# A mixture-of-experts layer staged over three batches, with one ring of four PSUM banks

## The chip, the cores and the metric

The kernel runs on one core of one Trainium2 chip. The metric is the device time of one launch in microseconds (us), the median of several runs. Every number below is of that core: TensorE (PE; PEld is its weight load, which overlaps it), VectorE (DVE), ScalarE (ACT), GpSimd (POOL) and the DMA queue that SyncE (SP) feeds.

## What is computed

Four transformer layers in a row over 16 batches of 256 tokens of width 128, with a context of 1601 rows per batch. The first layer, the third and the fourth are attention layers; they run in two programs with the name prefixes `pa_` and `pb_`, and nothing of them is touched. The case is about the second layer, whose buffers begin with `moe_`. Cut to what matters:

```python
nx = _layer_norm(x, ln_gamma, ln_beta)
q = nx @ Wq ; k = prototype_bank @ Wk ; v = prototype_bank @ Wv      # bank: 1601 rows
weights = softmax(einsum('bth,bph->btp', q, k) * H ** (-0.5))
evidence = einsum('btp,bph->bth', weights, v)
combined = concatenate([nx, evidence, anchor], axis=-1)
router_probs = softmax(combined @ router_W + router_b)
h = silu(einsum('btc,ecr->bter', combined, e_w1) + e_b1)              # 3 experts, 256 hidden
expert_out = einsum('bter,erh->bteh', h, e_w2) + e_b2
routed = sum(expert_out * router_probs[..., None], axis=-2)
g = sigmoid(silu(combined @ gate_w1 + gate_b1) @ gate_w2 + gate_b2)
return x + g * (routed @ out_w + out_b)
```

## The kernel before

`expert_layer` works on one batch at a time in units; each unit is a few matmuls of PE into one PSUM bank and the move of that bank to SBUF by ACT or DVE. Tokens come as two tiles (QT = 2) of 128, the context as 13 tiles of 128 rows (the last has 65), in four groups of at most four tiles.

The front of a batch is: `ln` (layer norm statistics on DVE, with the inverse root by 15 small operations, L155 to L168, and `xn`, L1319), `xt` (two transposes, L1536), `q` (L1539) and `qk` (times Wk transposed, L1542), `c0` to `c3` (transposes of the context, L1548), `s0` and `s1` (scores of token tile 0 and 1 in four banks of 400 columns, L1528; row maxima on DVE, L1333; exponentials on ACT, L1456; then sum, reciprocal and a diagonal matrix of the reciprocals, L1339 to L1345), `p00` to `p13` (probabilities transposed and divided at once by a matmul with that diagonal, L1564, moved by L1421 on ACT and L1255 on DVE), `pc` (context times probabilities, 13 accumulating matmuls, L1554) and `ev` (times Wv, L1557).

The back is: `r` (router logits, L1575, softmax on DVE and ACT, L1359 to L1372), `h0` to `h2` (an expert's hidden layer, L1580; ACT reads the bank as `hz`, L1480, takes the tanh, L1483, and DVE multiplies, L1382), `g1` (L1583), `e0` and `e1` (the experts' second matmuls for one token tile, L1589, each expert with a bias matmul of one row, L1590; DVE weights and adds, L1399 and L1401), `g2` (L1594, bias L1595; tanh L1487, then L1407 on DVE), `rt` (two transposes, L1600), `o` (L1604, bias L1605; DVE multiplies by the gate, L1412; POOL adds x, L1506; SP stores, L1285).

The front uses two banks in turn, the back two others. Every engine walks one list in program order: `walk` puts the front of batch b+1 between the units of the back of batch b, so two batches are in flight. The exponentials of a token tile stand right behind its scores on ACT, and its maxima, sum and diagonal in one piece on DVE. x has three buffers, the context one (`cin`), the probabilities before the transpose one per token tile.

A wait names a unit's count on a semaphore: `f_full` and `b_full` count what PE has filled, `f_free` and `b_free` what has been moved out.

## Time and profile before

| | us |
|---|---|
| median of 3 runs | 5992.55 |
| lowest and highest | 5966.28, 6003.84 |
| the profiled execution | 5973.85 |
| its span on the core | 5972.1 |

The span has three parts: the program `pa_` up to about 1978 us, the expert layer from there to 2834 us, and the program `pb_`. Over the whole span PE is busy for 84%, DVE for 68%, ACT for 62% and POOL for 27%. Only the middle part is changed. A busy PE is not PE at its peak, since the ends of matmuls are modelled and a weight load or a drain can stand between two of them: the difference between two starts is the better price. A float32 matmul shows as two instructions, a transpose as one.

### The profile page before, as it was taken

The numbers are of one execution on the slowest core, as the hardware profiler recorded it, in microseconds if no ns is written. First come the engines' busy times: TensorE is split into PE (matmuls) and PEld (weight loads), VectorE is DVE, ScalarE is ACT, GpSimd is POOL, SyncE is SP. The second block draws the span as 40 slices with busy tenths as digits, with TensorE's granted clock in tenths as the row PEclk, the third lists the DMA queues.
The fourth block names the chain that finished last, engine by engine and source line by source line (L and its number), as shares of the span: only waits on it lengthen the run. The fifth ranks groups of instructions, "written<-read, shape, count | busy, mean of one in ns | idle before, by whom it ended". The sixth has DMA issues, their size and how long they took to land.

```text
span 5972.1 us, 124563 instructions
## 1 busy us (share of the span) xinstructions
PE 5013.7 (84%) x48593; PEld 2443.0 (41%) x48593; DVE 4034.0 (68%) x8799; ACT 3691.2 (62%) x5043; POOL 1624.9 (27%) x2594
## 2 busy tenths in 40 slices
PE   3688888888888688888598888888888898888887
PEld 1233333333433466666233333333334343333333
DVE  3487877777776233332588878787877777777774
ACT  1376767667767233332277777777777777777775
POOL 2434343343321000000423232323222322322321
PEclk8699999999999788888699999999999999999998
DMA  1221111211110100000211212121212111111110
GB/s 42 60 61 46 51 53 50 59 43 47 51 34 24 34 16 22 23 23 17 68 43 58 60 50 61 50 61 50 61 50 62 48 51 44 52 49 42 53 42 7
DMA packets 362968, 271.18 MB, mean 45 GB/s; under 512 B 47905, under 2 KB 324990, under 8 KB 362384
## 3 DMA queue, kind: packets, MB, share of 16 engines
q1 hardware_dynamic: 362384, 263.23, 15.5%
q8 instruction: 387, 6.34, 0.4%
q14 instruction: 197, 1.61, 0.1%
HBM read 86.96 MB, written 12.78 MB: 17 GB/s over the span
## 4 chain that ended last, share of the span: by engine, by line
PE 31%; DVE 8%; ACT 6%; POOL 4%; issue 4%; SPq 0%; DMA 0%; ACTq 0%; POOLq 0%
PE pb_obank L914 11%; PE pb_dbank L927 7%; DVE pb_c_maxs L599 6%; ACT pb_probs L668 4%; PE pb_aunit L890 4%; PE pb_aunit L961 2%; PE pb_aunit L968 2%; POOL pb_c_cin L789 1%; PE pb_aunit L1001 1%; PE pb_dbank L975 1%; DVE pb_z_maxs L599 1%; POOL pb_c_hg L852 1%; PE pb_aunit L995 1%; POOL pb_c_cs_y L785 0%; ACT pb_c_ksp L712 0%
## 5 line engine op out<-in xcount | busy, mean ns | idle before, releaser
L599 DVE TENSOR_REDUCE pb_c_maxs<-pb_dbank 128x1 f32<-128x512 f32 (+1 forms) x3584 | 2050.6, 627 | 633.3 <-PE pb_dbank L927 621.2
L668 ACT ACTIVATE pb_probs<-pb_aunit 128x1024 f32<-128x1024 f32 (+1 forms) x1792 | 1756.0, 1025 | 460.7 <-PE pb_aunit L890 364.6
L599 DVE TENSOR_REDUCE pa_c_maxs<-pa_dbank 128x1 f32<-128x512 f32 (+1 forms) x1792 | 1028.6, 627 | 395.6 <-PE pa_dbank L927 390.4
L668 ACT ACTIVATE pa_probs<-pa_aunit 128x1024 f32<-128x1024 f32 (+1 forms) x960 | 943.0, 1025 | 263.6 <-PE pa_aunit L890 190.8
L927 PE MATMUL pb_dbank<-pb_c_kst,pb_c_qst 62*128 62x512 bf16 (+1 forms) x4096 | 880.1, 343 | 141.5 <-DVE pb_c_maxs L599 77.0
L914 PE MATMUL pb_obank<-pb_probs,pb_c_vaug 128*9 128x256 f32 x13312 | 890.2, 382 | 6.6 <-ACT pb_probs L668 6.5
L890 PE MATMUL pb_aunit<-pb_c_qst,pb_c_kst 64*128 64x256 bf16 x6144 | 595.8, 273 | 53.3 <-ACT pb_probs L668 21.9
L927 PEld LDWEIGHTS pb_dbank<-pb_c_kst,pb_c_qst 62*128 62x128 bf16 x4096 | 248.6, 93 | 778.4 <-DVE pb_c_maxs L599 563.7
L927 PE MATMUL pa_dbank<-pa_c_kst,pa_c_qst 62*128 62x512 bf16 (+1 forms) x2048 | 449.0, 354 | 61.5 <-DVE pa_c_maxs L599 24.2
L914 PE MATMUL pa_obank<-pa_probs,pa_c_vaug 128*9 128x256 f32 x6656 | 461.2, 393 | 0.8 <-ACT pa_probs L668 0.7
L914 PEld LDWEIGHTS pb_obank<-pb_probs,pb_c_vaug 128*9 128x9 f32 x13312 | 276.1, 90 | 371.9 <-issue 177.3
L890 PEld LDWEIGHTS pb_aunit<-pb_c_qst,pb_c_kst 64*128 64x128 bf16 x6144 | 258.6, 95 | 242.0 <-ACT pb_probs L668 84.4
L890 PE MATMUL pa_aunit<-pa_c_qst,pa_c_kst 64*128 64x256 bf16 x3072 | 300.9, 278 | 25.7 <-ACT pa_probs L668 16.7
L927 PEld LDWEIGHTS pa_dbank<-pa_c_kst,pa_c_qst 62*128 62x128 bf16 x2048 | 123.3, 95 | 390.0 <-DVE pa_c_maxs L599 257.1
L599 DVE TENSOR_REDUCE pa_z_maxs<-pa_dbank 128x2 f32<-128x512 f32 x256 | 164.1, 686 | 115.3 <-PE pa_dbank L927 113.9
L1506 POOL TENSOR_TENSOR moe_xo<-moe_y,moe_xin 128x256 f32<-128x256 f32 x16 | 11.6, 723 | 844.2 <-DVE moe_y L1412 844.2
L914 PEld LDWEIGHTS pa_obank<-pa_probs,pa_c_vaug 128*9 128x9 f32 x6656 | 140.2, 91 | 195.7 <-issue 101.7
L803 POOL TENSOR_TENSOR pb_c_kf<-pb_c_kf,pb_c_ksp 128x1024 f32<-128x1024 f32 x64 | 114.3, 1787 | 311.1 <-ACT pb_c_ksp L712 311.1
L890 PEld LDWEIGHTS pa_aunit<-pa_c_qst,pa_c_kst 64*128 64x128 bf16 x3072 | 129.1, 96 | 117.3 <-ACT pa_probs L668 44.2
L599 DVE TENSOR_REDUCE pb_z_maxs<-pb_dbank 128x2 f32<-128x512 f32 x256 | 164.6, 685 | 10.5 <-PE pb_dbank L927 8.7
L1564 PE MATMUL moe_bank_f<-moe_diag,moe_pr 128*128 128x128 f32 (+1 forms) x832 | 136.9, 320 | 35.5 <-DVE moe_pt L1255 28.5
L1456 ACT ACTIVATE moe_pr<-moe_bank_s,moe_nm 128x400 f32<-128x400 f32 (+1 forms) x128 | 74.3, 594 | 132.5 <-DVE moe_nm L1337 132.5
(460 smaller groups left out, 6864.7 us busy)
## 6 DMA issues: line engine op xcount, KB each, us to landing
pb_c_kst<-pb_c_ksp SPq DMA_DIRECT2D x384, 200.1 KB
pa_c_kst<-pa_c_ksp SPq DMA_DIRECT2D x192, 200.1 KB
pb_c_cin<-in_ctx SPq DMA_DIRECT2D x32, 768.0 KB
pa_c_cin<-in_ctx SPq DMA_DIRECT2D x16, 768.0 KB
moe_cin<-in_ctx SPq DMA_DIRECT2D x16, 768.0 KB
pb_c_qst<-pb_c_qsp SPq DMA_DIRECT2D x384, 32.0 KB
...
```

Of the source, the lines that this page charges most:

```text
L599: dve.tensor_reduce(dst, dbank[N % RING_D][:, 0:cnt * width].rearrange("p (s c) -> p s c", s=cnt), AX.X, ALU.max).then_inc(d_free, 1)
L668: act.activation(probs[u % RING_P][0:rows].rearrange("p a i q -> p (a i q)"), src[0:rows, :], ACT.Exp, scale=HD ** -0.5).then_inc(a_free, 1)
L789: pool.tensor_scalar(s.cin[0:rows, t, :], s.cin[0:rows, t, :], s.cs_m[0:rows, t:t + 1], s.cs_y[0:rows, t:t + 1], ALU.add, ALU.mult).then_i ...
L803: pool.tensor_tensor(s.kf[:, part], s.kf[:, part], s.ksp[:, 0, part], ALU.subtract).then_inc(s.k_r, 1)
L852: pool.tensor_tensor(s.hg[:], s.hg[:], s.z[:], ALU.mult).then_inc(s.g_p, 1)
L890: ins = pe.matmul(dst[:, par * 512 + h * NQ:par * 512 + (h + 1) * NQ], s.kst[b2][lo:lo + ROWS, pair, t * P:(t + 1) * P], s.qst[b2][lo:lo + ...
L914: ins = pe.matmul(obank[32 * h4:32 * h4 + HD + 1, half * NQ:(half + 1) * NQ], s.vaug[i % 2][:, t, 4 * q + h4, :], src, start=(t == 0), sto ...
L927: ins = pe.matmul(dbank[nd[tok, s.key, i, par] % RING_D][:, col:col + width], s.qst[b2][lo:lo + MAX_ROW, p, qt * P:(qt + 1) * P], s.kst[b2 ...
L961: ins = pe.matmul(dst[:, at - t0 * P:at - t0 * P + width], w.wkp[:], src[:, at:at + width], start=True, stop=True)
L968: ins = pe.matmul(dst[0:rows, (t - t0) * P:(t - t0 + 1) * P], (s.srct if s.has_ctx else s.xmt)[:, t * P:t * P + rows], w.wv[:], start=True ...
L1456: act.activation(pr[qt][:, at:at + width], sbank[c][:, 0:width], ACT.Exp, bias=nm[:, qt:qt + 1], scale=D ** -0.5, accum_out=sums[:, qt, c: ...
L1564: ins = pe.matmul(dst[0:rows, (t - t0) * P:(t - t0 + 1) * P], pr[qt][:, t * P:t * P + rows], diag[qt][:], start=True, stop=True)
```

## The change

The expert layer has a new list of stages, `expert_stages`, which all engines walk. In the body numbered b, a token (name, offset) works on batch b + offset: `xt`, `qk`, `c`, the scores `s` and the exponentials of token tile 0 (`x`, 0) on batch b+2; the exponentials of token tile 1 (`x`, 1), `p`, `dn`, `rb`, `pc` and `ev` on b+1; the back on b; `ln` on b+3. There are 19 bodies, the first and the last only partly filled.

- All units use one ring of four banks in turn, 27 uses for each batch; a unit waits until the use four before it has been moved. Each score bank is still apart.
- `q` is gone: Wq times Wk transposed is made once, and `qk` is one matmul from `nxt`.
- `p` is a plain transpose of unscaled probabilities. `dn` makes sum, reciprocal and diagonal for both token tiles at once; `rb` is two matmuls of a matrix of ones with the diagonals, which spreads the reciprocals over all rows (`recb`); the product `pc` is multiplied by it as DVE moves it.
- The biases of `e`, `g2` and `o` are split once, by `bias_parts` on DVE, in three bf16 parts in rows 0, 32 and 64 of `brows`. One bf16 matmul over 384 or 256 columns opens each bank in place of the six or two matmuls of one row.
- The inverse root is one power on POOL, which also makes `xn` and the affine step of `g2`.
- x has five buffers, the context three, the probabilities two, `nxt` three. The loads of the context are issued before the second part of the constants, and from then on after the product of three batches earlier.
- The softmax of the router is split: the exponential stands ahead of `hz` of expert 1 on ACT, the rest ahead of DVE's part of it.

```diff
+def expert_stages(nb, groups):
+
+    plan = [("xt", 2), ("p", 1, 0, 0), ("h", 0, 0), ("qk", 2), ("x", 1, 1), ("p", 1, 0, 1), ("dn", 1), ("r", 0), ("h", 0, 1),
+            ("c", 2, 0), ("p", 1, 0, 2), ("p", 1, 0, 3), ("rb", 1), ("h", 0, 2), ("c", 2, 1), ("p", 1, 1, 0), ("c", 2, 2),
+            ("g1", 0), ("p", 1, 1, 1), ("c", 2, 3), ("s", 2, 0), ("p", 1, 1, 2), ("p", 1, 1, 3), ("e", 0, 0), ("e", 0, 1), ("g2", 0),
+            ("x", 2, 0), ("ln", 3), ("pc", 1), ("s", 2, 1), ("rt", 0), ("ev", 1), ("o", 0)]
+    out = []
+    for b in range(-3, nb):
+        for tok in plan:
+            n = b + tok[1]
+            if 0 <= n < nb:
+                out.append((tok[0], tok[2:], n))
+    return out
...
-    FRONT = ["xt", "q", "qk", "c0", "c1", "c2", "c3"] + [f"p{qt}{g}" for qt in range(QT) for g in range(len(TG))] + ["pc", "ev"]
-    BACK = ["r", "h0", "h1", "h2", "g1", "e0", "e1", "g2", "rt", "o"]
...
+    RING = ("xt", "qk", "c", "p", "rb", "pc", "ev", "r", "h", "g1", "e", "g2", "rt", "o")
+    nu = {}
+    for k, arg, n in PROG:
+        if k in RING:
+            nu[k, arg, n] = len(nu)
...
-        wq, wk, wkt, wv = (sb(n, [P, D]) for n in ("wq", "wk", "wkt", "wv"))
+        wq, wk, wqt, wkt, wqk, wv = (sb(n, [P, D]) for n in ("wq", "wk", "wqt", "wkt", "wqk", "wv"))
...
+        xin = [sb(f"xin{i}", [P, QT, D]) for i in range(5)]
+        cin = [sb(f"cin{i}", [P, KT, D]) for i in range(3)]
...
-        pr = [sb(f"pr{i}", [P, KEYS]) for i in range(QT)]
-        sums, tot, rec = sb("sums", [P, QT, NCH]), sb("tot", [P, QT]), sb("rec", [P, QT])
+        pr = [[sb(f"pr{j}{i}", [P, KEYS]) for i in range(QT)] for j in range(2)]
...
+        recb = sb("recb", [P, NQ])
...
+        def filled(k, arg, n):
+
+            return u_full, nu[k, arg, n] + 1
+
+        def moved(k, arg, n):
+
+            N = nu[k, arg, n]
+            return u_free[N % RING_U], N // RING_U + 1
...
+            for dst, src, slow in consts_list[0:6]:
+                sp.dma_start(dst, src, allow_slow_non_contiguous=slow).then_inc(consts, 16)
             load_c(0)
+            for dst, src, slow in consts_list[6:]:
+                sp.dma_start(dst, src, allow_slow_non_contiguous=slow).then_inc(consts, 16)
             load_x(1)
+            load_c(1)
+            for part in range(3):
+                row = 32 * part
+                sp.dma_start(braw[row:row + 1, 0:EXPERTS, :], w["e_b2"].rearrange("(o e) n -> o e n", o=1)).then_inc(b_in, 16)
+                sp.dma_start(braw[row:row + 1, EXPERTS, :], w["gate_b2"].rearrange("(o n) -> o n", o=1)).then_inc(b_in, 16)
+                sp.dma_start(braw[row:row + 1, EXPERTS + 1, :], w["out_b"].rearrange("(o n) -> o n", o=1)).then_inc(b_in, 16)
...
+                load_c(n + 3)
                 store(n)
+                load_x(n + 4)
+                load_cols(n + 2)
...
+            def bias_parts():
+                dve.wait_ge(b_in, 9 * 16)
+                dve.wait_ge(b_zero, 1)
+                link = Chain(dve, b_step, 0)
+                for part in range(3):
+                    row = slice(32 * part, 32 * part + 1)
+                    src = braw
+                    for _ in range(part):
+                        link(dve.tensor_copy(bpart[row], src[row]))
+                        link.join()
+                        link(dve.tensor_tensor(brest[row], src[row], bpart[row], ALU.subtract))
+                        link.join()
+                        src = brest
+                    dve.tensor_copy(brows[row, 0:EXPERTS + 1, :], src[row, 0:EXPERTS + 1, :]).then_inc(b_set, 1)
+                    dve.tensor_copy(brows[row, EXPERTS + 1, :], src[row, EXPERTS, :]).then_inc(b_set, 1)
+                    for t in range(QT):
+                        dve.tensor_copy(brows[row, EXPERTS + 2 + t, :], src[row, EXPERTS + 1, :]).then_inc(b_set, 1)
...
+                    if n == 0:
+                        bias_parts()
...
+                elif k == "dn":
+                    dve.wait_ge(s_exp, (n + 1) * QT * NCH)
+                    if n:
+                        dve.wait_ge(*filled("rb", (), n - 1))
+                    dve.tensor_reduce(tot[:], sums[n % 2][:], AX.X, ALU.add).then_inc(s_sum, 1)
+                    dve.wait_ge(s_sum, n + 1)
+                    dve.reciprocal(rec[:], tot[:]).then_inc(s_rec, 1)
+                    dve.wait_ge(s_rec, n + 1)
+                    for qt in range(QT):
+                        dve.tensor_scalar(diag[qt][:], ident[:], rec[:, qt:qt + 1], None, ALU.mult).then_inc(s_diag, 1)
...
+                elif k == "pc":
+                    dve.wait_ge(*filled(k, arg, n))
+                    dve.wait_ge(*moved("rb", (), n))
+                    if n:
+                        dve.wait_ge(*filled("ev", (), n - 1))
+                    dve.tensor_tensor(pct[:], src[:, 0:NQ], recb[:], ALU.mult).then_inc(free, 1)
...
+                elif k in ("h", "g1"):
+                    j = arg[0] if k == "h" else EXPERTS
+                    if j == 1:
+                        link = Chain(dve, r_dve, n * R_PER)
+                        link.n = 2
+                        dve.wait_ge(r_exp, n + 1)
+                        link(dve.reduce_sum(ls[:], le[:], AX.X))
+                        link.join()
+                        link(dve.reciprocal(ls[:], ls[:]))
+                        link.join()
+                        link(dve.tensor_tensor(rp[:], le[:], ls[:].unsqueeze(2).to_broadcast([P, QT, EXPERTS]), ALU.mult))
+                        link.join()
+                    dve.wait_ge(h_tanh, HIDDEN * n + j + 1)
...
+                elif k == "x":
+                    qt = arg[0]
+                    act.wait_ge(s_neg, n * QT + qt + 1)
+                    if n >= 2:
+                        act.wait_ge(*filled("p", (qt, len(TG) - 1), n - 2))
+                        act.wait_ge(s_sum, n - 1)
+                    for c, (at, width) in enumerate(CH):
+                        act.activation(pr[n % 2][qt][:, at:at + width], sbank[c][:, 0:width], ACT.Exp, bias=nm[:, qt:qt + 1], scale=SCALE,
+                                       accum_out=sums[n % 2][:, qt, c:c + 1]).then_inc(s_exp, 1)
...
+                elif k in ("h", "g1"):
+                    j = arg[0] if k == "h" else EXPERTS
+                    if j == 1:
+                        act.wait_ge(r_dve, n * R_PER + 2)
+                        wait(act, r_dve, n * R_PER)
+                        act.activation(le[:], lx[:], ACT.Exp).then_inc(r_exp, 1)
+                    if j == 0:
+                        act.wait_ge(cols_in[n % 2], (n // 2 + 1) * COL_LOADS)
+                    act.wait_ge(*filled(k, arg, n))
+                    wait(act, h_out, HIDDEN * n + j)
...
+                if k == "ln":
+                    pool.wait_ge(ln_st, 2 * QT * (n + 1))
+                    pool.tensor_scalar(rs_v[:], ag[:, :, 1], EPS, None, ALU.add).then_inc(ln_p, 1)
+                    pool.tensor_scalar(rs_m[:], ag[:, :, 0], -1.0, None, ALU.mult).then_inc(ln_p, 1)
+                    pool.wait_ge(ln_p, 3 * n + 2)
+                    pool.tensor_tensor(rs_y[:], rs_v[:], mhalf[:], ALU.pow).then_inc(ln_p, 1)
+                    pool.wait_ge(ln_p, 3 * n + 3)
+                    if n:
+                        pool.wait_ge(*filled("xt", (), n - 1))
+                    for t in range(QT):
+                        pool.tensor_scalar(xn[:, t, :], xin[n % 5][:, t, :], rs_m[:, t:t + 1], rs_y[:, t:t + 1], ALU.add, ALU.mult).then_inc(x_ln, 1)
...
+            for k, arg, n in PROG:
+                if k in RING:
+                    N = nu[k, arg, n]
+                    dst = ubank[N % RING_U]
+                    wait(pe, u_free[N % RING_U], N // RING_U)
...
+                    pe.wait_ge(*moved("xt", (), n))
+                    ins = pe.matmul(dst[:, 0:NQ], wqk[:], nxt[n % 3][:], start=True, stop=True)
...
+                elif k == "p":
+                    qt, g = arg
+                    t0, cnt = TG[g]
+                    pe.wait_ge(s_exp, (n * QT + qt + 1) * NCH)
+                    for t in range(t0, t0 + cnt):
+                        rows = LAST if t == KT - 1 else P
+                        ins = pe.transpose(dst[0:rows, (t - t0) * P:(t - t0 + 1) * P], pr[n % 2][qt][:, t * P:t * P + rows], ident[:])
+                elif k == "rb":
+                    pe.wait_ge(s_diag, (n + 1) * QT)
+                    for qt in range(QT):
+                        ins = pe.matmul(dst[:, qt * P:(qt + 1) * P], ones[:], diag[qt][:], start=True, stop=True)
...
-                    wait(pe, s_norm, after(n, QT, qt))
-                    for t in range(t0, t0 + cnt):
-                        rows = LAST if t == KT - 1 else P
-                        ins = pe.matmul(dst[0:rows, (t - t0) * P:(t - t0 + 1) * P], pr[qt][:, t * P:t * P + rows], diag[qt][:], start=True, stop=True)
...
+                elif k == "e":
+                    qt = arg[0]
+                    pe.wait_ge(b_set, 12)
+                    pe.wait_ge(h_out, HIDDEN * n + EXPERTS)
+                    pe.matmul(dst[:, 0:EXPERTS * D], ones_b[:], brows[:, 0:EXPERTS, :].rearrange("p e d -> p (e d)"), start=True, stop=False)
                     for e in range(EXPERTS):
                         for r in range(2):
-                            pe.matmul(dst[:, e * D:(e + 1) * D], hh[:, e, r, qt * P:(qt + 1) * P], ew2[:, e, r, :], start=(r == 0), stop=False)
-                        ins = pe.matmul(dst[:, e * D:(e + 1) * D], ones[:], eb2[0:1, e, :], start=False, stop=True)
+                            ins = pe.matmul(dst[:, e * D:(e + 1) * D], hh[:, e, r, qt * P:(qt + 1) * P], ew2[:, e, r, :], start=False, stop=(e == EXPERTS - 1 and r == 1))
```

## Rows read from the trace of the kernel before

**Rows 1.** Fifteen periods in one window: us, busy times and instructions, granted clock, DMA share, GB/s
```profile
2080.00:2830.00 750.00, 634.59 (x2962) 491.63 (x2962) 260.52 (x879) 230.91 (x589) 10.85 (x15) 0.87 0.08 21
```
**Rows 2.** The tile moe_y: durations of 16 instructions in ns, first and last start
```profile
L1412 DVE TENSOR_TENSOR moe_y<-moe_bank_g,moe_g x16: 424/425/426, 2080.0 to 2830.0; 128x256 f32<-128x256 f32 x16
```
**Rows 3.** PE's longest wait of one period: us, times, longest
```profile
PE moe_bank_s L1528 <- DVE moe_ct L1326: 2.1, 1, 2.1
```
**Rows 4.** Windows of one period, columns as in rows 1
```profile
2290.00:2297.00 7.00, 6.01 (x19) 4.89 (x20) 0.98 (x6) 1.04 (x3) 0.09 (x1) 0.53 0.61 156
2297.00:2324.00 27.00, 21.77 (x113) 16.19 (x111) 14.15 (x49) 12.34 (x32) 0.00 (x0) 1.00 0.00 1
```
**Rows 5.** Timeline, PE in one period: start us, us, engine, line, operation, instructions
```profile
2281.51 5.85 PE L1554 MATMUL moe_bank_f<-moe_pt,moe_cin 128*128 128x256 f32 x26 [0.47 <-DVE moe_pt L1257]
...
2299.92 1.04 PE L1548 MATMUL moe_bank_f<-moe_ident,moe_cin 128*128 128x128 f32 x8
...
2300.79 0.60 PE L1580 MATMUL moe_bank_g<-moe_nxt,moe_ew 128*128 128x256 f32 x2
...
2305.39 2.93 PE L1528 MATMUL moe_bank_s<-moe_ct,moe_qk 128*128 128x401 f32 x8 [2.06 <-DVE moe_ct L1326]
...
2313.83 0.61 PE L1589 MATMUL moe_bank_g<-moe_ew,moe_hh 128*128 128x128 f32 x4
...
2314.37 0.48 PE L1590 MATMUL moe_bank_g<-moe_eb,moe_ones 1*128 1x128 f32 x2
...
2314.79 0.71 PE L1589 MATMUL moe_bank_g<-moe_ew,moe_hh 128*128 128x128 f32 x4
...
2328.79 2.05 PE L1564 MATMUL moe_bank_f<-moe_diag,moe_pr 128*128 128x128 f32 x16
...
2330.68 0.38 PE L1600 MATMUL moe_bank_g<-moe_ident,moe_rt 128*128 128x128 f32 x2
```
**Rows 6.** Timeline, ACT and DVE around scores and a hidden layer, same columns
```profile
2297.57 0.84 ACT L1480 ACTIVATE moe_hz<-moe_bank_g,moe_acols 128x256 f32<-128x256 f32 x2 [2.91 <-PE moe_bank_g L1580]
...
2298.44 0.63 ACT L1483 ACTIVATE moe_ht<-moe_hz 128x512 f32<-128x512 f32 x1
...
2299.17 0.69 DVE L1382 SCALAR_TENSOR_TENSOR moe_hh<-moe_ht,moe_hz 128x512 f32<-128x512 f32 x1 [6.05 <-ACT moe_ht L1483]
...
2306.40 2.53 DVE L1333 TENSOR_REDUCE moe_mx<-moe_bank_s 128x1 f32<-128x401 f32 x4 [1.27 <-PE moe_bank_s L1528]
...
2309.34 0.60 ACT L1456 ACTIVATE moe_pr<-moe_bank_s,moe_nm 128x401 f32<-128x401 f32 x1 [5.07 <-DVE moe_nm L1337]
...
2311.64 0.48 ACT L1475 ACTIVATE moe_gz<-moe_bank_g,moe_acols 128x256 f32<-128x256 f32 x1
```
**Rows 7.** Timeline, the router's small operations
```profile
2082.28 0.17 DVE L1359 TENSOR_TENSOR moe_lg<-moe_bank_g,moe_rrow 128x6 f32<-128x6 f32 x1 [1.85 <-PE moe_bank_g L1575]
...
2083.06 0.21 ACT L1466 ACTIVATE moe_le<-moe_lx 128x6 f32<-128x6 f32 x1 [2.04 <-DVE moe_lx L1365]
```
**Rows 8.** DVE's move of a bank over the fifteen periods: busy us, mean ns, idle before
```profile
L1255 DVE COPY moe_pt<-moe_bank_f 128x512 f32<-128x512 f32 x28 | 19.2, 686 | 11.7 <-PE moe_bank_f L1564 11.7
```
**Rows 9.** Timeline, bf16 matmuls in the program pa
```profile
1003.86 0.64 PE L927 MATMUL pa_dbank<-pa_c_kst,pa_c_qst 62*128 62x512 bf16 x2
1004.29 0.42 PE L927 MATMUL pa_dbank<-pa_z_kst,pa_z_qst 62*128 62x256 bf16 x1
```
**Rows 10.** The normalization's line on POOL in the program pb
```profile
L778 POOL TENSOR_SCALAR pb_c_xn<-pb_c_xin,pb_c_rs_m,pb_c_rs_y x64: 447/449/452, 2864.9 to 5704.2; 128x128 f32<-128x128 f32 x64
```
**Rows 11.** Timeline, the layer's beginning, its last operations, and what follows
```profile
1978.69 0.34 SPq L1263 DMA_DIRECT2D moe_ident<-in_ident  x1
...
1990.55 0.47 PE L1514 MATMUL moe_bank_g<-moe_ident,moe_wk 128*128 128x128 f32 x1 [17.87 <-DMA moe_ew<-in_L_xcond_e_w]
...
2028.98 0.38 ACT L1421 ACTIVATE moe_pct<-moe_bank_f 128x256 f32<-128x256 f32 x1 [6.05 <-PE moe_bank_f L1554]
...
2834.11 0.35 SPq L464 DMA_DIRECT2D pb_ident<-in_ident  x1
```

More of the change, by code:

```diff
@@ L1488, in back @@
                 elif k == "rt":
-                    wait(act, b_full, after(d, UB, i))
-                    wait(act, b_full, after(d - 1, UB, B_AT["o"]))
-                    copy(rtt[:], src[:, 0:NQ]).then_inc(freed, 1)
-            walk(act, front, back)
+                    act.wait_ge(*filled(k, arg, n))
+                    if n:
+                        act.wait_ge(*filled("o", (), n - 1))
+                    copy(rtt[:], src[:, 0:NQ]).then_inc(free, 1)
         @block.gpsimd
         def _(pool):
-            def front(k, n, w):
-                return
@@ new lines, in _ @@
+            pe.transpose(ubank[0][:, 0:P], wq[:], ident[:]).then_inc(turned, 1)
+            pe.transpose(ubank[1][:, 0:P], wk[:], ident[:]).then_inc(turned, 1)
+            pe.wait_ge(turned, 4)
+            pe.matmul(ubank[2][:, 0:P], wqt[:], wkt[:], start=True, stop=True).then_inc(turned, 1)
+            pe.wait_ge(turned, 6)
+            for k, arg, n in PROG:
+                if k in RING:
+                    N = nu[k, arg, n]
+                    dst = ubank[N % RING_U]
+                    wait(pe, u_free[N % RING_U], N // RING_U)
+                if k == "s":
+                    qt = arg[0]
+                    if qt == 0:
+                        pe.wait_ge(*moved("qk", (), n))
+                        for g in range(len(TG)):
+                            pe.wait_ge(*moved("c", (g,), n))
@@ L1596, in back @@
                 elif k == "rt":
-                    for key in ("e0", "e1"):
-                        wait(pe, *b_done(d, B_AT[key]))
+                    for qt in range(QT):
+                        pe.wait_ge(*moved("e", (qt,), n))
                     for t in range(QT):
```

464 lines of the change are left out of this document (193 added, 271 removed).

## The prediction

> **What bounds the kernel now.** I read the timeline at both ends of the expert layer first, since nothing else is changed: its first transfer is issued at 1978.7 us and the next program's first at 2834.1 us [rows 11], so the layer takes 855.4 us of the 5973.85 us of the profiled execution. All the rest stays as it is. Within it, the start of the last product by the gate recurs every (2830.0 - 2080.0) / 15 = 50.0 us [rows 2]: a period per batch, with 40 to 50 us of filling ahead of it. Next the windows: over fifteen periods PE is busy 634.6 of 750 us, DVE 260.5, ACT 230.9 [rows 1]. PE bounds the layer, with two leaks. It stands idle (750 - 634.6) / 15 = 7.7 us of each period, of which the longest wait, of `s0` for DVE's move of the last context bank, is 2.1 us [rows 3]. And its granted clock is 0.87: it falls to 0.53, which is 1.2 GHz for nearly the whole stretch, for some 7 us behind the product, in `o`, `ev`, `r` and the waits among them, and is at 2.4 GHz from 2297 to 2324 [rows 4]. A mean of 0.87 is (1 - 0.87) x 2 = 26% of the time, 13 us of a period, at the lower clock, which costs up to 6.5 us of each 50.
>
> **Prices of PE at 2.4 GHz** from the differences of starts [rows 5]. A transpose: (2300.79 - 2299.92) / 8 = 0.11 us. A matmul with a diagonal, two instructions: (2330.68 - 2328.79) / 8 = 0.24 us. One of 256 columns: 26 instructions are 13 matmuls in 5.85 us with the tail, 0.43 us each. Four scores of 400 columns: 2.93 us with the tail, 2.67 in a row. Two second matmuls of an expert: 2314.37 - 2313.83 = 0.54 us; its bias of one row: 2314.79 - 2314.37 = 0.42 us.
>
> **The change on PE, per batch.** (1) 26 transposes in place of 26 matmuls: 26 x 0.13 = 3.4 us less. (2) `q` goes: 0.43 less. (3) `rb` comes: two matmuls, 0.53 more. (4) Biases: six of one row in `e0` and `e1` (2.5 us), two in `g2`, two in `o` (1.7 us), together 4.2 us, replaced by four bf16 matmuls. No float32 row beside it has 384 bf16 columns, so it has bounds: below, 512 columns take (1004.29 - 1003.86) / 2 = 0.22 us [rows 9]; above, the old price per 128 columns stays, and nothing is saved. I take 0.22, since the work is one pass of the kind of rows 9, and add 0.1 for the change of shape of the array: So e0 and e1 are 2 x (6 x 0.25 + 0.32) = 3.6 us where they take 6.3 now (three times 0.54 + 0.42 each and the tail), g2 and o 2 x (2 x 0.25 + 0.32) = 1.6 where they take 3.3: 4.4 less. Sum of PE's work before: xt 0.3, q and qk 0.9, c 1.6, scores 5.3, p 6.8, pc 5.6, ev 0.4, r 0.9, hidden 5.1, g1 0.9, e 6.3, g2 and o 3.3, rt 0.3, together 37.7. With 7.7 idle and 6.5 for the clock that gives 52, where 50.0 is measured: the method is 4% high. After: 37.7 - 3.4 - 0.4 + 0.5 - 4.4 = 30.0 us; the walk below, unit by unit, comes to 29.6.
>
> **The other engines.** DVE loses the inverse root and `xn` (about 3 us) and gains 0.4 for the scaled product; it has 17.4 us in 50 now [rows 1] and some 15 after. ACT stays at about 15 (q and pct go, rb comes). Both lie beneath 30. POOL gets 0.45 us for each token tile of `xn` [rows 10] and small steps, 2.5 to 3 us, a third of a body ahead of its reader, and the affine step of `g2` (about 0.9 from the same row), which ends before `o`. If POOL were late, `xt` and behind it the whole list would wait; it has over 10 us of cover. The context load may start when the product of three batches earlier is done, a whole body ahead of `c`; SP stands behind each store, which ends a body, so about 30 us remain. These edits I cost at nothing.
>
> **What waits now.** With one list and one ring, the question is which move is late. I walked one body with the prices above and these: scores to the first exponential 2309.34 - 2305.39 = 3.95 us, four exponentials 2.3 us, hidden bank to freed 0.84, then tanh 0.63 and DVE's product 0.69 [rows 6], a bank of 512 columns 0.60 on ACT as the first exponential there, 0.69 on DVE [rows 8], router to its exponential 0.78 [rows 7]. PE to reader is 0.28 us, reader to PE 0.1. Time 0 is the start of `s0`:
> PE does s0, p, p, e0, e1, g2 without a stop to 7.6, pc to 13.1, s1 to 15.8, rt, ev, then 0.3 of wait for rt's copy, o, xt, p, h0 to 19.9, qk to 20.35, p, r, h1 to 23.45, c0, p to 24.45. ACT frees h0 at 21.0, takes its tanh, moves qk, and only then, at 21.9, begins the exponentials of tile 1; they end at 24.2. DVE stands in `dn` for them and makes the diagonals until 25.2; behind `dn` in its queue are `r`, `h1`'s product and a p bank. So `r` is moved at 25.45 (PE waits 1.05 for that bank), the router's exponential on ACT is at 26.0, and h1 is freed at 26.95, where `rb` waits for its bank: 1.4 us. ACT's next move, c0, is behind h1's tanh and ends at 28.1: h2 waits 0.6. Then h2's tanh and DVE's product let c1 be moved at 33.0 (p11 waits 0.9) and c3 at 34.8 (the next s0 waits 1.2). The waits are 5.2 to 5.4 us, and the body is 35.0 us at full clock.
>
> **The clock.** The low stretch that now follows the product becomes shorter, since the one-row biases go. But from 23.45 to 28.2 and from 29.9 to 34.95 PE has waits and transposes, and a matmul for less than 1 us in each. Falls to 1.2 GHz are likely there. With 6 to 9 us of a body at the lower clock (now 13), of which part passes in waits, I add 3 us: 38 us. Both ends: nothing, 35; and every unit but scores, product and second matmuls at half clock, 14.4 us more work less the 5.3 us of waits that absorb it, 44.
>
> **The sum.** Filling: constants and the first context now come first; before, PE began at 1990.55, 11.9 us in, and I add 3 us for the context's bytes ahead of the rest. Two bodies without a back take some 22 us each (before, the first front alone ended its product 2028.98 - 1990.55 = 38.4 us behind PE's start [rows 11]); DVE's bias work of 7 us lies in the first of them and is in the 22. So 59 us. Fourteen bodies with back, middle and front: 14 x P. The last two, without front and without middle, 27 and 20 us with store and hand-over. New layer: 106 + 14 P; whole: 5973.85 - 855.4 + 106 + 14 P = 5224 + 14 P. At P = 38 that is 5756. The profiled execution lies 19 us under the median of 5992.55, so the same gain from the median is 5775. I give 5765.
>
> **The rivals.**
> - *Clock stays high* (P = 35): 5714. For it: the stretch from 2297 to 2324 holds the wait of 2.1 us [rows 3] and stays at 1.00 [rows 4]. Against it: that wait is followed by dense work, the new ones by transposes. 0.22.
> - *Transposes don't hold the clock* (P = 44): 5840. 26 + 13 + 4 transposes a body replace a third of the dense matmuls of now. Against it: 8 transposes at 2299.92 ran at full clock, but among the hidden layers. 0.17. The Trainium skill, TensorE: Matmul & The Clock Gate, Part 4, says of transposes that "HAM K=8/8 doesn't engage for transpose-mode", the full clock; by that rule this is the outcome, and the rows neither show nor exclude it.
> - *Waits vanish* (P = 30): the exponentials of tile 1 come sooner than I walked, and PE alone bounds: 5644. Against it: two engines must each be ahead at five places. 0.06.
> - *Head of line* (P = 48): with in-order moves one late operation holds up all four banks, and each of the waits above doubles and draws a lower clock along: 5896. 0.05.
> - *The other side: half clock throughout.* If so many transposes and waits keep PE at 1.2 GHz, the work is 2 x 30 = 60 us a body: 5224 + 840 + some 30 in the ends = 6094. It decides from P = (5973.85 - 5224) / 14 = 53.6 us. Against it: scores and product are dense for 8 us in a row at 7.6 to 15.8. 0.03.
>
> **How the numbers follow.** Forecast 0.47, around P = 36.5 to 40.5, 5735 to 5800; the others as given, together 1. The range reaches from the high clock (5714, less 10 for the spread of the runs) to the lower clock over transposes (5840): 5705 to 5845, with the filling and the bias bounds (4 us a body at most) in it. A measurement of this kernel can tell about 1% from no change, 60 us, which is P = 49.3. Faster by over 1%: 0.95. Within 1%: 0.02, the upper end of the head-of-line case. Slower: 0.03.
>
> **What would show it.** The start of the gate's product should recur every 36 to 40 us, PE's waits sum to 5 to 6 us a body, the longest at `rb`, at p03 for the router's bank and at s0; L1564's successor should cost 0.11 to 0.13 us per tile and a bias matmul under 0.3. Clock around 0.88. I am wrong if the clock of the stretch from r to c3 is low in every body (period 44), if PE's waits exceed 8 us, or if a gap of over 2 us stands ahead of pc or xt.

## The result: 5721.9 us, and the profile after

| | before | after |
|---|---|---|
| median, us | 5998.19 (4 runs) | 5721.87 (4 runs) |
| lowest and highest | 5966.28, 6018.63 | 5696.35, 5724.06 |
| the profiled execution | 5973.85 | 5719.91 |
| expert layer in it, first issue to the next program's first | 855.4 | 582.7 |
| period, mean of twelve full bodies | 52.0 | 34.1 |

The ratio is 0.953, 95% interval 0.9501 to 0.9559. Predicted were 5765, with 5705 to 5845 as the range: the forecast is 43 us too high, and the range holds the time, while the 5735 to 5800 that the forecast gave to its own case does not. The two profiled executions differ by 254 us and their expert layers by 273. The rest lies in the two programs around it, whose text is the same: `pb_` took 3138 us in the one and 3162 in the other, `pa_` 1979 and 1974. The medians differ by 276 us, close to the layers.

Four views of the profile after. First, the timeline of SP and PE at the ends of the layer (start us, us, engine, line, operation), which answers to [rows 11]:

```profile
1973.58 0.38 SPq L1262 DMA_DIRECT2D moe_xin<-x_after  x1
...
1986.33 0.48 PE L1555 MATMUL moe_bank_u<-moe_ident,moe_wq 128*128 128x128 f32 x1 [18.78 <-DMA moe_ew<-in_L_xcond_e_w]
...
2556.32 0.35 SPq L464 DMA_DIRECT2D pb_ident<-in_ident  x1
```

Second, POOL's last addition of each body, which marks the period; the first, some of the middle, and the last three of sixteen:

```profile
2065.89 0.73 POOL L1549 TENSOR_TENSOR moe_xo<-moe_y,moe_xin 128x256 f32<-128x256 f32 x1 [6.64 <-DVE moe_y L1446]
...
2202.09 0.73 POOL L1549 TENSOR_TENSOR moe_xo<-moe_y,moe_xin 128x256 f32<-128x256 f32 x1 [6.64 <-DVE moe_y L1446]
2235.81 0.73 POOL L1549 TENSOR_TENSOR moe_xo<-moe_y,moe_xin 128x256 f32<-128x256 f32 x1 [6.64 <-DVE moe_y L1446]
2270.74 0.73 POOL L1549 TENSOR_TENSOR moe_xo<-moe_y,moe_xin 128x256 f32<-128x256 f32 x1 [6.64 <-DVE moe_y L1446]
...
2509.24 0.72 POOL L1549 TENSOR_TENSOR moe_xo<-moe_y,moe_xin 128x256 f32<-128x256 f32 x1 [9.44 <-DVE moe_y L1446]
2535.23 0.73 POOL L1549 TENSOR_TENSOR moe_xo<-moe_y,moe_xin 128x256 f32<-128x256 f32 x1 [7.08 <-DVE moe_y L1446]
2552.66 0.72 POOL L1549 TENSOR_TENSOR moe_xo<-moe_y,moe_xin 128x256 f32<-128x256 f32 x1 [2.07 <-DVE moe_y L1446]
```

There are two kinds of bodies: 2235.81 - 2202.09 = 33.72 us, and 2270.74 - 2235.81 = 34.93, which comes about every third time. The last two take 25.99 and 17.43. Third, the windows of the thirteen periods between 2065.9 and 2509.2, of one period of the shorter kind, and of 4 us in the longer kind (columns as in [rows 1]), and fourth PE's waits in the thirteen (us in total, times, longest):

```profile
2065.90:2509.20 443.30, 388.22 (x2146) 313.88 (x2146) 199.09 (x568) 197.34 (x521) 39.68 (x86) 0.98 0.11 31
2202.00:2235.80 33.80, 29.48 (x168) 23.89 (x167) 15.36 (x45) 15.37 (x41) 3.22 (x7) 1.00 0.13 34
2244.00:2248.00 4.00, 3.67 (x11) 2.90 (x12) 0.98 (x3) 2.03 (x5) 0.00 (x0) 0.57 0.00 0
```
```profile
PE moe_bank_s L1574 <- DVE moe_ct L1355: 14.8, 13, 1.1
PE moe_bank_u L1601 <- ACT moe_hz L1510: 13.5, 13, 1.0
PE moe_bank_u L1597 <- DVE moe_lg L1392: 11.0, 13, 1.0
PE moe_bank_u L1597 <- DVE moe_ct L1355: 9.7, 13, 0.7
PE moe_bank_u L1622 <- ACT moe_ct L1453: 4.1, 10, 0.4
```

PE is idle for (443.3 - 388.2) / 13 = 4.2 us of a body, the granted clock is 0.98 where it was 0.87 [rows 1], and PE waits at the five places that the walk named and hardly anywhere else. DVE and ACT are busy for 15.3 and 15.2 us of a body. The twelve full periods of the kernel before, in one window:

```profile
2080.51:2704.99 624.48, 527.45 (x2461) 409.42 (x2460) 221.00 (x756) 192.16 (x492) 8.68 (x12) 0.87 0.08 22
```

There PE is idle for (624.5 - 527.5) / 12 = 8.1 us of a period. So 52.0 us = 37.7 work by the prediction's prices + 8.1 idle, with 6.2 left for the clock, became 34.1 = 29.5 work, as in the shorter kind, + 4.2 idle + 0.4. Of the 17.9 us, some 8.2 are PE's work, 3.9 its waits, and the remainder of 5.8 the clock.

### The profile page after: what moved, and what is told of

The parts are those of the page before. It is cut to its first block, busy times and chain, and to the rows that moved or that the text cites. A ratio compares the mean times of both kernels' runs of the same rounds, so it can differ in the third digit from the quotient of the medians.

```text
span 5718.1 us, 123215 instructions
## 1 busy us (share of the span) xinstructions
PE 4820.5 (84%) x47956; PEld 2303.5 (40%) x47956; DVE 3989.6 (70%) x8517; ACT 3680.6 (64%) x5027; POOL 1669.9 (29%) x2691
## 4 chain that ended last, share of the span: by engine, by line
PE 32%; DVE 8%; ACT 6%; POOL 4%; issue 4%; SPq 0%; DMA 0%; ACTq 0%; POOLq 0%
PE pb_obank L914 12%; PE pb_dbank L927 8%; DVE pb_c_maxs L599 6%; ACT pb_probs L668 4%; PE pb_aunit L890 4%; PE pb_aunit L961 2%; PE pb_aunit L968 2%; POOL pb_c_cin L789 1%; PE pb_aunit L1001 1%; PE pb_dbank L975 1%; DVE pb_z_maxs L599 1%; POOL pb_c_hg L852 1%; PE pb_aunit L995 1%; POOL pb_c_cs_y L785 1%; ACT pb_c_ksp L712 1%
## 5 line engine op out<-in xcount | busy, mean ns | idle before, releaser
L815 POOL CAST pb_c_mbf<-pb_c_negm 128x16 bf16<-128x16 f32 x64 | 12.7, 198 | 411.0 <-DVE pb_c_negm L604 411.0
L961 PE MATMUL pb_aunit<-pb_c_srct,pb_l_cross_wkp 128*128 128x512 f32 (+1 forms) x256 | 122.6, 609 | 7.8 <-ACT pb_probs L668 7.8
```

Source lines behind the costliest of these rows:

```text
L961: ins = pe.matmul(dst[:, at - t0 * P:at - t0 * P + width], w.wkp[:], src[:, at:at + width], start=True, stop=True)
```

## Experiments

Each gives the length of the layer and the mean of twelve full periods, read from a profiled execution as above; a ratio is of medians to the kernel before. The programs on either side take from 5106 to 5145 us together in these executions, so periods are the finer measure.

**Transposes in a row, and matmuls in a row.** Do transposes hold the clock? In the changed kernel, ahead of every `pc` and into its bank, which `pc` then overwrites:

```diff
                     for t in range(QT):
                         for g in range(len(TG)):
                             pe.wait_ge(*moved("p", (qt, g), n))
+                    for t in range(120):
+                        pe.transpose(dst[:, 0:P], cin[n % 3][:, t % 12, :], ident[:])
```

and in its twin 55 float32 matmuls of the same shape in their place.

> The changed kernel with a run of 120 more transposes of context tiles ahead of each product, into the bank that the product then overwrites. Theory 1 (plain transposes hold the clock as matmuls do): 120 x 0.11 = 13.2 us a body more, period 47.3, clock 0.97 or more. Theory 2 (they do not): the clock falls inside the run, transposes there take 0.2 us each, the run 20 to 26 us, and the period is 55 or more.

> The changed kernel with a run of 55 more float32 matmuls of the same size and operands, 110 instructions, in the same place. Both theories: clock stays high, 55 x 0.24 = 13.2 us a body, period 47.3. It is the yardstick for the run of transposes.

Measured (one execution of each): periods 47.8 and 47.3 us, clock 0.97 in both. The run of transposes in PE's timeline, a window within it (columns as in [rows 1]), and then the run of matmuls in the other kernel:

```profile
2216.23 13.26 PE L1607 MATMUL moe_bank_u<-moe_ident,moe_cin 128*128 128x128 f32 x120
2229.33 5.78 PE L1610 MATMUL moe_bank_u<-moe_pt,moe_cin 128*128 128x256 f32 x26
```
```profile
2220.00:2224.00 4.00, 4.00 (x39) 4.00 (x38) 0.00 (x0) 0.00 (x0) 0.10 (x1) 1.00 0.00 0
```
```profile
2210.17 12.45 PE L1607 MATMUL moe_bank_u<-moe_ident,moe_cin 128*128 128x128 f32 x110
2222.45 5.78 PE L1610 MATMUL moe_bank_u<-moe_pt,moe_cin 128*128 128x256 f32 x26
```

120 transposes take (2229.33 - 2216.23) = 13.1 us, 0.11 each, and PE is granted 2.4 GHz during all of them. 55 matmuls take 12.3, 0.22 each. A run of transposes entered at the full clock stays there. The Trainium skill, TensorE: Matmul & The Clock Gate, Part 4, says that the full clock doesn't engage for transposes; these rows disagree for a run of float32 transposes of 128x128 that is entered at the full clock, and there the measurement decides. The rival of 5840 us falls. No run here shows whether transposes alone would bring a fallen clock back.

**The biases alone, from both sides.** In the changed kernel, the ten one-row matmuls back in place of the four bf16 ones:

```diff
-                    pe.matmul(dst[:, 0:EXPERTS * D], ones_b[:], brows[:, 0:EXPERTS, :].rearrange("p e d -> p (e d)"), start=True, stop=False)
                     for e in range(EXPERTS):
                         for r in range(2):
...
+                        ins = pe.matmul(dst[:, e * D:(e + 1) * D], ones[0:1, :], braw[0:1, e, :], start=False, stop=True)
```

and the reverse in the kernel before, where bf16 parts are the only edit.

> The changed kernel, but the biases are again float32 matmuls of one row, ten a batch, in place of the four bf16 ones. Theory 1 (work): 4.4 us more a body, period about 38.5, 65 to 70 us more in all. Theory 2 (the one-row matmuls are also what let the clock fall behind the product before): the clock falls again near e and o, to 0.93 or lower over the layer, and the period comes to 40 or more. Rival: under 2 us a body.

> The kernel before with one part of the change alone: biases split in three bf16 parts, four bf16 matmuls a batch for ten of one row. Theory 1 (work on the path): period 50.0 to about 45.6, some 70 us less. Theory 2 (the one-row matmuls in o let the clock fall behind the product): the granted clock of the layer rises from 0.87 to above 0.93 and the period comes under 44. Rival (the waits of the old two pairs of banks take it): DVE's moves are late instead, and the period stays above 48.

Measured: biases back, ratio 0.9715 (0.9678 to 0.9753), layer 693.5 us, period 41.0, which is 6.8 more. bf16 parts in the old order: ratio 0.9901 (0.9867 to 0.9934), layer 804.9, period 49.5, which is 2.6 less. That is the expectation's rival: the clock rises from 0.87 to 0.90 only, and PE is idle for 11.8 us of a period in place of 8.1. The same block in both forms, first in the changed kernel, then with the biases back:

```profile
2221.72 0.33 PE L1630 MATMUL moe_bank_u<-moe_brows,moe_ones_b 96*128 96x384 bf16 x1
2221.89 1.50 PE L1633 MATMUL moe_bank_u<-moe_ew,moe_hh 128*128 128x128 f32 x12
2223.22 0.33 PE L1630 MATMUL moe_bank_u<-moe_brows,moe_ones_b 96*128 96x384 bf16 x1
...
2224.73 0.28 PE L1636 MATMUL moe_bank_u<-moe_brows,moe_ones_b 96*128 96x256 bf16 x1
...
2225.29 5.78 PE L1608 MATMUL moe_bank_u<-moe_pt,moe_cin 128*128 128x256 f32 x26
```
```profile
2256.98 0.61 PE L1632 MATMUL moe_bank_u<-moe_ew,moe_hh 128*128 128x128 f32 x4
2257.52 0.48 PE L1633 MATMUL moe_bank_u<-moe_braw,moe_ones 1*128 1x128 f32 x2
2257.93 0.71 PE L1632 MATMUL moe_bank_u<-moe_ew,moe_hh 128*128 128x128 f32 x4
2258.57 0.48 PE L1633 MATMUL moe_bank_u<-moe_braw,moe_ones 1*128 1x128 f32 x2
...
2263.21 0.49 PE L1637 MATMUL moe_bank_u<-moe_gw,moe_g 128*128 128x128 f32 x2
...
2264.87 5.88 PE L1608 MATMUL moe_bank_u<-moe_pt,moe_cin 128*128 128x256 f32 x26
```

`e0` and `e1` take 2224.73 - 2221.72 = 3.0 us against 2263.21 - 2256.98 = 6.2, `g2` 0.56 against 1.66. Not only does the one-row bias cost 0.41 us (2257.93 - 2257.52): the two matmuls behind it take 0.64 (2258.57 - 2257.93), where in an unbroken run of twelve instructions, six matmuls, two take (2223.22 - 2221.89) / 3 = 0.44. With `o` taken like `g2`, the bias edit is 3.2 + 1.1 + 1.1 = 5.4 us of PE's work. Of the 1.4 us left to 6.8, some 0.8 is the stretch at 1.2 GHz, which now comes in every body and not in every third; 0.6 stays open. That stretch stands where it stood, at `rb` and `h2`, and not near `e` and `o`, as theory 2 had it; the clock is 0.96.

**Plain transposes alone, from both sides.** In the changed kernel `p` by a matmul with the identity, two instructions each; in the kernel before `p` by transposes, with the division by the sum left out, so that the probabilities there stay unscaled.

```diff
-                        ins = pe.transpose(dst[0:rows, (t - t0) * P:(t - t0 + 1) * P], pr[n % 2][qt][:, t * P:t * P + rows], ident[:])
+                        ins = pe.matmul(dst[0:rows, (t - t0) * P:(t - t0 + 1) * P], pr[n % 2][qt][:, t * P:t * P + rows], ident[:], start=True, stop=True)
```

> The changed kernel, but the probabilities are turned by a float32 matmul with the identity in place of the plain transpose: 26 x 0.13 = 3.4 us more PE work a body. Theory 1 (PE's work is what the transposes saved): period 34.1 plus 2.5 to 3.4, since up to 0.9 may pass in the waits at p03 and p11; 40 to 55 us more in all. Theory 2 (transposes let the clock fall, and dense matmuls hold it): the granted clock of the layer rises from 0.98 to 1.00 and gives 0.4 us back. Rival (the plain transposes were hidden in waits): the period moves by less than 1 us.

> The kernel before with plain transposes of the probabilities alone; the division by the sum is left out, so the evidence is unscaled. Theory 1 (work on the path): 3.4 us less a period, 46.6, some 54 us less in all. Rival 1 (DVE and ACT move those banks as slowly as before and bound that stretch): under 1 us. Rival 2 (transposes don't hold the clock): the clock falls below 0.87 and the gain is under 1.5 us.

Measured: matmuls in the new order, ratio 0.9549 (0.9511 to 0.9587), layer 596.6, period 35.2, every body the same, clock 1.00. Transposes in the old order, ratio 1.0023 (1.0002 to 1.0044), layer 859.7, period 52.3: nothing gained. The changed kernel loses little without the transposes because its waits take up the work: the wait at p03 is gone and that at p11 is 0.3 in place of 0.7, and the stretch at 1.2 GHz is gone too. So of 26 x 0.11 = 2.9 us of work only 1.0 to 1.4 is seen. A window of 400 us with matmuls (columns as in [rows 1]), and a window of the old order with transposes:

```profile
2110.00:2510.00 400.00, 367.00 (x2170) 305.10 (x2171) 177.17 (x498) 175.32 (x452) 35.36 (x77) 1.00 0.11 29
```
```profile
2257.00:2273.00 16.00, 15.53 (x53) 12.38 (x54) 7.89 (x33) 2.45 (x5) 0.00 (x0) 0.50 0.00 0
```

In the second PE is busy for 15.5 of 16 us at 1.2 GHz, with second matmuls, biases and transposes mixed. The stretch begins behind a wait of 1.2 us at a `p`. Over 400 us the clock there is 0.83, where the kernel before has 0.87. So in the old order the 3 us of work saved go in part to waits (9.3 us of a period idle, 1.2 more) and in the larger part, some 2 us, to the clock. Both are named by the expectation, the clock as its rival 2. Its reason, that transposes don't hold the clock, is not borne out by the run of 120; why the clock is lower here stays open, and whether a stretch already at 1.2 GHz ends later with transposes in it was not tested.

**Both unit edits in the old order.** The two edits of the kernel before together, division left out as above. Is the old order able to use them?

> The kernel before, in its old order, with both edits of units: bf16 parts for the biases, and plain transposes of the probabilities in place of the matmul with the diagonal. The division by the sum is left out, so that the probabilities stay unscaled. Alone they moved the period from 52.0 to 49.5 and to 52.3 us. Theory (in the old order the waits and the clock take the gain): 49 to 50.5 us, layer 800 to 820 us, clock 0.86 to 0.90, whole 5920 to 5950; the new order, ring and buffers are then worth 15 us of the 17.9 of a period. Rival (they add once both are there): 7.8 us less work of PE gives 44 to 46 us, layer 725 to 755 us, whole 5850 to 5880.

Measured: ratio 0.9881 (0.9854 to 0.9908), layer 806.8, period 49.4, clock 0.85. PE's work is 7.8 us less by the prediction's terms, and the period 2.6 less. The waits of 400 us, and rows of the timeline (PE, ACT and DVE) of one period:

```profile
PE moe_bank_f L1595 <- DVE moe_pt L1259: 25.6, 9, 4.0
PE moe_bank_f L1595 <- ACT moe_pt L1452: 22.7, 8, 2.8
```
```profile
2251.48 0.60 ACT L1487 ACTIVATE moe_pr<-moe_bank_s,moe_nm 128x401 f32<-128x401 f32 x1 [2.80 <-DVE moe_nm L1368]
...
2253.77 0.61 ACT L1452 ACTIVATE moe_pt<-moe_bank_f 128x512 f32<-128x512 f32 x1
...
2254.43 1.12 PE L1595 MATMUL moe_bank_f<-moe_ident,moe_pr 128*128 128x128 f32 x4 [2.84 <-ACT moe_pt L1452]
...
2258.30 0.60 DVE L1348 TENSOR_SCALAR moe_xn<-moe_xin,moe_ag,moe_rs_y 128x128 f32<-128x128 f32 x2
...
2259.86 0.68 DVE L1259 COPY moe_pt<-moe_bank_f 128x512 f32<-128x512 f32 x1
...
2260.59 0.82 PE L1595 MATMUL moe_bank_f<-moe_ident,moe_pr 128*65 128x128 f32 x5 [2.43 <-DVE moe_pt L1259]
```

Here most of the gain goes: PE is idle for 12.5 us of a period in place of 8.1, and the granted clock is 0.85 where it was 0.87. A bank of `p` is moved on ACT only behind the four exponentials of the other token tile (2251.48 to 2253.77), and on DVE only behind `ln` with its inverse root and `xn` (from 2254.52 to 2258.90) and the weighting of `e0`; PE, with two banks for the front, waits 2.8 and 2.4 us. A faster unit only reaches these moves sooner. The new list spreads them: the exponentials of tile 0 stand a body ahead of their readers, those of tile 1 nine units ahead of theirs, and the root and `xn` are on POOL. Together with the four banks, the buffers of three batches and the missing `q` it is worth 49.4 - 34.1 = 15.3 us of a period, against 2.6 of the unit edits alone. The new list with both old units was not run, and which part is the root's was not run by itself. But the wait behind it stands in the kernel before already, in each of the twelve full periods, where the root and `xn` fill DVE from 2319.20 to 2322.79, and the move of `p` follows at 2323.74, behind the weighting of `e0`:

```profile
PE moe_bank_f L1564 <- DVE moe_pt L1255: 24.4, 12, 2.0
```

**Three banks in the ring.** `RING_U = 3` in the changed kernel.

> The changed kernel with three banks in the ring in place of four. Theory 1 (the depth of the ring hides the moves): every unit waits for the move three before; the waits at p03, rb, h2, p11 and s0 come one unit earlier, and xt and o wait too: 3 to 6 us more a body, period 37 to 40. Rival (the order alone hides the moves and the fourth bank is spare): the period stays within 0.5 us of 34.1.

Measured: 5741.02 us (one execution), layer 630.2, period 37.5, 3.3 more; clock 0.95. The wait at s0 grows from 1.1 to 1.9 and `g1` gets a wait of its own; in all PE is idle for 6.0 us of a period, 1.8 more, and the stretch at 1.2 GHz comes in every body:

```profile
PE moe_bank_s L1574 <- DVE moe_ct L1355: 21.0, 11, 1.9
PE moe_bank_u L1625 <- DVE moe_ct L1355: 14.7, 11, 1.3
```

**The exponentials earlier.** The walk says that `r` is late since DVE waits for the exponentials of tile 1, which stand behind `h0` on ACT. Put them first:

```diff
-    ... ("p", 1, 0, 0), ("h", 0, 0), ("qk", 2), ("x", 1, 1), ("p", 1, 0, 1) ...
+    ... ("p", 1, 0, 0), ("x", 1, 1), ("h", 0, 0), ("qk", 2), ("p", 1, 0, 1) ...
```

> The changed kernel with one token moved in the list of stages: the exponentials of token tile 1 stand ahead of expert 0's hidden layer, no longer behind qk. Theory 1 (the waits of the body are the chain exponentials of tile 1 - diagonals - router bank - hidden layer 1): ACT can begin them at 18.6 us of the body where it begins at 21.9, so PE's waits at the p03 bank (0.84 us) and at rb (1.04 us) go, and part of the one at h2 (0.4): period 34.1 to about 32.0 us, some 30 us less in all. Rival (a move put off only moves the wait): expert 0's bank is freed 2.3 us later, h1 and c0 wait for it, and the period stays at 33.7 to 34.5.

Measured: ratio 0.9492 (0.9464 to 0.952), layer 578.7, period 34.1 as before: 33.4 at full clock, but five of twelve bodies are long ones of 35.0, against four. That is the expectation's rival, that the waits only move. The wait at p03 is gone, that at `rb` is not, and a new one of 0.3 stands at `h1`. The timeline shows what is late now:

```profile
2242.89 0.69 DVE L1419 SCALAR_TENSOR_TENSOR moe_hh<-moe_ht,moe_hz 128x512 f32<-128x512 f32 x1 [4.57 <-ACT moe_ht L1513]
...
2244.89 0.16 DVE L1392 TENSOR_TENSOR moe_lg<-moe_bank_u,moe_rrow 128x6 f32<-128x6 f32 x1
...
2245.59 0.82 ACT L1510 ACTIVATE moe_hz<-moe_bank_u,moe_acols 128x256 f32<-128x256 f32 x2
...
2246.46 0.71 PE L1601 MATMUL moe_bank_u<-moe_diag,moe_ones 128*128 128x128 f32 x4 [1.04 <-ACT moe_hz L1510]
```

The exponentials are done, but the router's logits still stand on DVE behind `h0`'s product, the move of p01 (from 2243.50) and `dn` (from 2244.10), and ACT's move of `h1` behind the router's exponential.

**The waits by changes of order.** Three kernels, each with the moves of the one before it. `a_r_early` puts `r` and the exponentials ahead of `h0`; `a_order2` puts also c1 ahead of `h2` and c3 ahead of p11; `a_order3` also `dn` ahead of `h0` and c3 ahead of `g1`:

```diff
-    plan = [("xt", 2), ("p", 1, 0, 0), ("h", 0, 0), ("qk", 2), ("x", 1, 1), ("p", 1, 0, 1), ("dn", 1), ("r", 0), ("h", 0, 1),
-            ("c", 2, 0), ("p", 1, 0, 2), ("p", 1, 0, 3), ("rb", 1), ("h", 0, 2), ("c", 2, 1), ("p", 1, 1, 0), ("c", 2, 2),
-            ("g1", 0), ("p", 1, 1, 1), ("c", 2, 3), ("s", 2, 0), ("p", 1, 1, 2), ("p", 1, 1, 3), ("e", 0, 0), ("e", 0, 1), ("g2", 0),
+    plan = [("xt", 2), ("p", 1, 0, 0), ("r", 0), ("x", 1, 1), ("dn", 1), ("h", 0, 0), ("qk", 2), ("p", 1, 0, 1), ("h", 0, 1),
+            ("c", 2, 0), ("p", 1, 0, 2), ("p", 1, 0, 3), ("rb", 1), ("c", 2, 1), ("h", 0, 2), ("p", 1, 1, 0), ("c", 2, 2),
+            ("c", 2, 3), ("g1", 0), ("p", 1, 1, 1), ("s", 2, 0), ("p", 1, 1, 2), ("p", 1, 1, 3), ("e", 0, 0), ("e", 0, 1), ("g2", 0),
```

> Only r and the exponentials of tile 1 ahead of h0, the rest as the changed kernel. Theory: the waits at p03 and rb (1.8 us) go, those at s0, p11 and h2 (2.2 us) stay; period 32.3 us, layer 550 to 560 us, ratio to the kernel before 0.944 to 0.947. Rival: the wait at rb stays near 1 us as with the exponentials alone (period 33.4 to 34.2), since DVE's other work ahead of it decides.

> Three moves in the list of the changed kernel: r and the exponentials of tile 1 ahead of h0; c1 ahead of h2; c3 ahead of p11. The period of the changed kernel is 34.1 us, with waits of 1.1 us at s0 for c3's move, 1.0 at rb for h1's move, 0.7 at p11 for c1's move, 0.4 at h2, and 0.8 at p03, which the earlier exponentials alone already took away. Theory (the waits are places in DVE's and ACT's queues, each can be taken out by its own move): h1's move no longer stands behind the router, so rb doesn't wait; c1 is moved ahead of the product of h2, c3 0.7 us sooner; the waits of a period fall to 1 us or less and the period is 30.5 to 32 us, the layer 535 to 550 us, the whole 5630 to 5660. Rival A (the waits only move): other banks come late, waits stay at 2 to 3 us in other places, period 32.5 to 33.5, whole 5670 to 5690. Rival B (clock): with the waits gone elsewhere the granted clock falls below 0.96 and the period stays at 34.

> From the list with the three moves, two more: dn stands ahead of h0, and c3 ahead of g1. There PE still waited 1.4 us of a 32.2 us period at s0, since c3's move stood on DVE behind g1's product, which waits for its tanh, and 0.5 us at rb for dn's diagonals, which stood behind h0's product and a move of p01. Theory (each wait is a place in DVE's queue): both go, full-clock periods are 29.6 to 30.0 us in place of 31.5, the mean 29.8 to 30.6, the layer 520 to 530 us in place of 548, the whole 5655 to 5670 us. Rival A (ACT is next): s0 waits for ACT's move of c2 and p11 for that of p10, and half of the gain is left: period 31, layer 535. Rival B (clock): denser full-clock bodies, but more bodies with a stretch at 1.2 GHz: mean 31.5 or more.

| | median, us | ratio, interval | layer | period |
|---|---|---|---|---|
| the changed kernel | 5721.87 | 0.953, 0.9501 to 0.9559 | 582.7 | 34.1 (33.7, 34.9) |
| `a_r_early` | 5689.48 | 0.9492, 0.9468 to 0.9516 | 552.6 | 32.3 (31.6, 33.3) |
| `a_order2` | 5685.67 | 0.9484, 0.9463 to 0.9505 | 548.6 | 32.2 (31.5, 33.2) |
| `a_order3` | 5659.87 | 0.9423, 0.939 to 0.9455 | 521.6 | 30.2 (30.15) |

The first move gave the period that was expected, 32.3 us, though the ratio of 0.9492 lies above the 0.944 to 0.947 of the expectation. It took out the wait at `h2` too. The next two, run together, didn't: 32.2 in place of 30.5 to 32, since c3 stood on DVE behind `g1`'s product even with its new place ahead of p11, and the wait at s0 grew to 1.5. PE's waits of 400 us in `a_order2`:

```profile
PE moe_bank_s L1574 <- DVE moe_ct L1355: 15.9, 11, 1.5
PE moe_bank_u L1601 <- DVE moe_diag L1376: 6.5, 12, 1.3
```

The last two moves were made for these two rows, and took them away. The only wait of PE of over 0.3 us in eleven periods of `a_order3`, and the window of the same:

```profile
PE moe_bank_u L1590 <- ACT moe_ct L1453: 4.8, 11, 0.4
```
```profile
2115.36:2447.22 331.86, 323.78 (x1818) 261.64 (x1817) 166.33 (x480) 165.56 (x441) 33.07 (x73) 1.00 0.13 34
```

PE is busy for 323.8 of 331.9 us at the full clock, and a period is 30.2 us, as expected: PE's work, 29.5, is all but reached. This version beats both kernels; it is 0.9423 / 0.953 = 0.989 of the changed one (each ratio against the kernel before on its own chip), 62 us by the medians and 61 by the layers.

## Why the prediction was right, and where it was not

- **What bounds before.** PE, its waits, its clock: confirmed. One number was read wrongly. 50.0 us was a mean over fifteen periods of [rows 2], of which the last two are 46.7 and 27.7 us; a full one is 52.0. The sum of 52 was not 4% high: it met the full period. Its parts are less exact: the 7.7 of waits is 8.1 in a full period, and the 6.8 for `p` is more than the 26 x 0.24 = 6.2 of its own price. The sum of the new layer does not use the 50.0.
- **PE's work.** 29.6 to 30.0 predicted, 29.5 measured. Within it the biases save 5.4 and not 4.4: the bf16 matmul of 384 columns is 0.17 us and that of 256 is 0.11, where 0.32 was taken for each, and a second matmul was priced 0.25, where it is 0.22 in a run. For the 0.1 that was added there for the change of shape no run shows a cost. The transposes save 26 x 0.11 = 2.9, not 3.4, by the 0.22 of a matmul in `a_p_matmul`. The two misses partly cancel.
- **The waits.** The walk gave p03 1.05, `rb` 1.4, `h2` 0.6, p11 0.9 and s0 1.2. Measured: 0.84, 1.0, 0.4, 0.7 and 1.1. Each place is right, and each a little too long: some 4.2 us in place of 5.2 to 5.4, and 33.7 us at full clock in place of 35.0. The early-exponentials kernel shows that the reason given for two of them was half of it: behind the exponentials stands DVE's own queue.
- **The clock: the step that failed.** "I add 3 us": measured is 0.4, since the body falls to 1.2 GHz only in `rb` and `h2`, for some 4 us of every third body. What happened is the first rival, the clock stays high, which said P = 35 and 5714; it had 0.22 against 0.47. The reason against it, that the new waits are followed by transposes and not by dense work, doesn't hold: the run of 120 transposes held the clock as the matmuls did. What the low stretches follow is only partly known. In the changed kernel they come behind the waits ahead of `rb`; where the waits are gone (`a_order3`) or in part filled with work (`a_p_matmul`), the clock is 1.00 over all full bodies. But the same waits stand in every body and only every third falls: here the 2 us ahead of the stretch in a longer body, and the same 2 us of the body before it, which has no stretch. The third row is the kernel before, where PE was busy for 2.5 of the 3 us ahead of a fall (the window behind it is in [rows 4]), with the product's end, `o`, its one-row biases and `ev`:

```profile
2242.00:2244.00 2.00, 0.33 (x2) 0.13 (x1) 1.45 (x10) 0.78 (x3) 0.00 (x0) 1.00 0.44 130
2208.28:2210.28 2.00, 0.34 (x2) 0.13 (x1) 1.45 (x10) 0.78 (x3) 0.00 (x0) 1.00 1.09 313
```
```profile
2287.00:2290.00 3.00, 2.46 (x12) 1.55 (x11) 0.42 (x1) 0.77 (x2) 0.63 (x1) 1.00 0.02 5
```

So a gap alone is not the cause, and what decides stays open. The forecast's 38 us of a body is 3.9 too high: 2.6 by the clock, 1.1 by the waits and the rest by work. That the range holds the time in spite of this is due to its lower end, which was drawn from the rival with the high clock.

- **Filling and ends.** 59 + 27 + 20 = 106 us predicted. 582.7 - 14 x 34.1 = 105.3 measured; PE begins 12.8 us behind the first issue, where 15 was taken, and the last two bodies are 26.0 and 17.4, or 47.1 with what follows the last, where 27 + 20 was taken.
- **The edits costed at nothing.** On PE's path POOL's steps and DVE's scaled product (0.42 us) are hidden, as said. But the root and `xn` leaving DVE was not worth nothing: in the old order they stand ahead of a move of `p`, for which PE waited 2.0 us in every period, and 2.4 once its units were faster. The saving was in the walk, which had them no longer in DVE's queue, without being named as a term; its size was not measured by itself.
- **The sum.** With P = 34.1 the formula gives 5224 + 477 = 5701 against the profiled execution of before. The measured 5719.9 holds the 24 us by which the program `pb_` was slower this time, less 5 by which `pa_` was faster; from the median of 5992.55 the formula gives 5720, and the median is 5721.9. That they agree within 2 us is chance, since the programs on either side vary by up to 39 us.
- **The signs that were named.** Of what should show, the places of the waits, the price of a transpose and that of a bias matmul came true. The period (34.1 and not 36 to 40), the waits (4.2 us and not 5 to 6) and the clock (0.98 and not around 0.88) did not.
